# Shared feed-forward with its features on the partitions, and router products placed between its products

## The reference

```python
# x: (16, 512, 256)
h = layernorm(x)
a = tanh(h @ WA.T); b = h @ WB.T              # 16 states
g = sigmoid(h @ Wg.T + bg); dx = h @ WD.T + bD
hs = scan(h_t = a_t * h_{t-1} + b_t)          # along the 512 tokens
x = x + (hs @ WC.T) * g + dx * (1 - g)

h2 = layernorm(x)
shared = (silu(h2 @ shared_gate_w) * (h2 @ shared_up_w)) @ shared_down_w   # 256 -> 256 -> 256
p, idx = top_k(softmax(h2 @ router_w), 2)     # 16 experts
routed = sum over the 2 chosen experts e of  p_e * (silu(h2 @ gate_w[e]) * (h2 @ up_w[e])) @ down_w[e]
out = x + routed + shared
```

## Time and profile before

| | |
|---|---|
| median of 3 runs | 772.59 us (772.11 to 775.65) |
| span of the profiled execution | 772.7 us (no time of its own is noted beside it) |
| part A, from the first gate product to the first transposed expert rows | 14.96 to 429.97 us |
| halves with front, back and tail | 14, from 61.60 to 388.40 us |
| TensorE (PE) busy | 601.8 us (78%) |
| VectorE (DVE) busy | 539.9 us (70%) |
| ScalarE (ACT) / GpSimd (POOL) busy | 321.6 / 368.3 us |
| mean granted TensorE clock | 0.918 of full |

### The profile page before, as it was taken

One profiled execution on the slowest core, in us unless ns is written; L12 is line 12 of the kernel. 1 busy time (PEld: TensorE's weight loads), 2 busy tenths in 40 slices (PEclk: granted clock), 3 DMA queues, 4 the chain that ended last, 5 costly groups with the idle time before them and its releaser, 6 DMA issues.

```text
span 772.7 us, 16380 instructions
## 1 busy us (share of the span) xinstructions
PE 601.8 (78%) x3710; PEld 499.9 (65%) x3741; DVE 539.9 (70%) x1660; ACT 321.6 (42%) x733; POOL 368.3 (48%) x516
## 2 busy tenths in 40 slices
PE   3689899999999999999974788988988988970000
PEld 2467777777778777778763677877877877750000
DVE  8778898888899988897866245545445444545776
ACT  4366455565555565555452233333333333330000
POOL 3214445654545644445647356556556656661000
PEclk9789999999999999999997699999999999995555
DMA  4994111110101111101114434434544444417998
GB/s 155 275 330 125 38 40 50 56 48 34 48 34 56 55 41 41 48 34 57 57 45 171 117 120 156 155 114 155 156 131 148 146 135 146 147 50 247 379 385 293
DMA packets 82806, 96.91 MB, mean 125 GB/s; under 512 B 10142, under 2 KB 74066, under 8 KB 82774
## 3 DMA queue, kind: packets, MB, share of 16 engines
q1 hardware_dynamic: 61270, 54.32, 23.3%
q0 software_dynamic: 13056, 33.84, 12.1%
q10 hardware_dynamic: 8448, 8.39, 3.1%
HBM read 52.04 MB, written 46.57 MB: 128 GB/s over the span
## 4 chain that ended last, share of the span: by engine, by line
PE 57%; issue 12%; DVE 9%; DMA 7%; ACT 3%; POOL 2%; SPq 1%; DVEq 1%; POOLq 0%; ACTq 0%
PE gd L600 14%; PE tr L398 8%; PE gu L405 5%; DMA raw_w<-expert_results 5%; PE tr L405 5%; PE gd L436 5%; PE dn L405 5%; PE gu L617 4%; PE dn L617 4%; PE cb L398 3%; PE misc L405 2%; PE misc L527 2%; DVE tokens L1293 1%; SPq L383 1%; DMA expert_rows<-row_buf,slot 1%
## 5 line engine op out<-in xcount | busy, mean ns | idle before, releaser
L1355 POOL DMA_INDIRECT expert_rows<-row_buf,slot x128 | 132.0, 1031 | 145.3 <-DVE slot L1011 107.2
L1423 POOL DMA_INDIRECT expert_results<-raw_w,row_ids x144 | 141.6, 983 | 67.9 <-issue 35.2
L600 PE MATMUL gd<-w_hi,bx 128*128 x576 | 112.0, 297 | 0.6 <-DVE bx L1235 0.6
L436 PE MATMUL gd<-wgd,xT 128*128 128x512 f32 x384 | 103.0, 405 | 4.6 <-DVE xT L936 4.6
L398 PE MATMUL tr<-ident,row_buf 128*128 128x128 f32 x416 | 64.6, 279 | 46.4 <-issue 32.9
L1235 DVE TENSOR_TENSOR bx<-tr,bx 128x512 fp32r<-128x512 f32 x72 | 49.8, 692 | 71.6 <-ACT bx L820 63.7
L398 PEld LDWEIGHTS tr<-ident,row_buf 128*128 128x128 f32 x416 | 49.1, 142 | 64.1 <-issue 57.8
L600 PEld LDWEIGHTS gd<-w_hi,bx 128*128 128x128 f32 x576 | 85.1, 192 | 3.1 <-issue 1.0
L820 ACT ACTIVATE bx<-tr 128x512 fp32r<-128x512 f32 x71 | 42.5, 599 | 101.2 <-PE tr L398 101.2
L436 PEld LDWEIGHTS gd<-wgd,xT 128*128 128x128 f32 x384 | 71.7, 196 | 18.9 <-DVE xT L936 3.1
L1254 DVE TENSOR_TENSOR raw_w<-gd,raw_w 128x256 f32<-128x256 f32 x72 | 30.6, 425 | 64.7 <-ACT raw_w L826 64.7
(11 more groups left out here) (155 smaller groups left out, 1250.0 us busy)
## 6 DMA issues: line engine op xcount, KB each, us to landing
row_buf<-expert_rows SPq DMA_DIRECT2D x144, 130.0 KB, 2.1
raw_w<-expert_results SPq DMA_DIRECT2D x32, 512.0 KB, 10.9
tokens<-in_x SPq DMA_DIRECT2D x16, 512.0 KB, 4.9
out<-tokens ACTq DMA_DIRECT2D x16, 512.0 KB, 7.1
expert_results<-raw_w,row_ids POOLq DMA_INDIRECT x144, 2.4
expert_rows<-fill_rows SPq DMA_DIRECT2D x17, 130.0 KB, 2.6
raw_w<-in_gate_w SPq DMA_DIRECT2D x16, 128.0 KB, 4.3
raw_w<-in_up_w SPq DMA_DIRECT2D x16, 128.0 KB, 4.4
```

Source lines behind the costliest of these rows:

```text
L436: pe.matmul(gd[j % 2][:], xT[a][:, c, j * P:(j + 1) * P], wgd[b][:, c, :], start=(a, b, c) == (0, 0, 0), stop=False)
L600: last = pe.matmul(bgu[p][:, h * 2 * F:(h + 1) * 2 * F], bx[a][:, p, (h * KC + c) * P:(h * KC + c + 1) * P], gate_up_w[b][:, bass.ds(at[h] ...
L1355: pool.indirect_dma_start(out=rows, out_offset=bass.IndirectOffsetOnAxis(ap=slot[:, q, choice, j:j + 1], axis=0), in_=row_buf[:, q, j, :], ...
L1423: pool.indirect_dma_start(out=results, out_offset=bass.IndirectOffsetOnAxis(ap=row_ids[:, at, h:h + 1], axis=0), in_=y[:, w, h, :], in_off ...
```

## The change

The inner values of the shared feed-forward are made with the 256 inner features on the partitions and the 512 tokens of the block moving. Weights are now the stationary operand: `shared_gate(c)` and `shared_up(c)` for the two feature tiles c, six matmuls of 512 columns each. Their product is already transposed for the down product, so the inner transposes go; `inner_hi` (ACT) and `inner_lo` (DVE) split it from the SBUF tile `inner`. Elementwise work goes by 128x512 instead of 128x256. The four down products of a block all run in the next half, two to a bank (`dn`, `gu`), and DVE adds two token tiles at once. In halves with a front the 16 router matmuls (32 columns moving, a 128x128 piece of `h2T` stationary) are issued between the twelve of `shared_gate(0)` and `shared_up(0)`. `ranks_of_block` comes after `shared_gate(1)`, `shared_up(1)` is last. The front transposes of a block are all made in the half before.

```diff
-            def inner_transposes(k, j):
-                pe.wait_ge(inner_ready, J * k + j + 1)
-                if j:
-                    pe.wait_ge(innerT_ready, J * k + j)
-                transposes(cb, 0, [inner[:, j % 2, c * P:(c + 1) * P] for c in range(KC)], th_done)
...
             def shared_down_of(k, j):
-                pe.wait_ge(innerT_ready, J * k + j + 1)
-                if known(k, 1) or j:
-                    pe.wait_ge(shared_added, J * k + j)
-                three_passes(dn[:, 0:D], lambda a, c: innerT[a][:, j % 2, c * P:(c + 1) * P],
+                if j == 0:
+                    pe.wait_ge(innerT_ready, 2 * k + 2)
+                at = (j % 2) * D
+                three_passes(shared_out[j // 2][:, at:at + D], lambda a, c: innerT[a][:, c, j * P:(j + 1) * P],
                              lambda b, c: wshd[b][:, c, :]).then_inc(dn_done, 1)
...
+                def shared_gate(c, between=None):
+
+                    if c:
+                        pe.wait_ge(silu_ready, 2 * k + 1)
+                    elif known(k, 1):
+                        pe.wait_ge(shared_added, 2 * k)
+                    three_passes(gu[:], lambda a, i: wsh[a][:, i, c * P:(c + 1) * P],
+                                 lambda b, i: h2T[b][:, i, :], between).then_inc(gate_done, 1)
+
+                def shared_up(c, between=None):
+
+                    if c:
+                        pe.wait_ge(inner_ready, 2 * k + 1)
+                    elif known(k, 1):
+                        pe.wait_ge(shared_added, 2 * k - 1)
+                    three_passes(dn[:], lambda a, i: wsh[a][:, i, D + c * P:D + (c + 1) * P],
+                                 lambda b, i: h2T[b][:, i, :], between).then_inc(up_done, 1)
...
+                        def with_gate(m):
+                            for step in router[m:m + 1] if m < 4 else router[2 * m - 4:2 * m - 2]:
+                                router_step(*step)
+
+                        def with_up(m):
+                            for step in router[8 + 2 * m:10 + 2 * m] if m < 2 else router[10 + m:11 + m]:
+                                last = router_step(*step)
+                                if step == router[-1]:
+                                    last.then_inc(router_done, 1)
+
+                        shared_gate(0, with_gate)
+                        shared_up(0, with_up)
...
+            def inner_hi(k, c):
+                act.wait_ge(inner_ready, 2 * k + c + 1)
+                if known(k, 1):
+                    act.wait_ge(dn_done, J * k)
+                act.activation(innerT[0][:, c, :], inner[:, c, :], ACT.Copy).then_inc(innerT_hi, 1)
...
+            def inner_lo(k, c):
+                dve.wait_ge(innerT_hi, 2 * k + c + 1)
+                dve.tensor_tensor(innerT[1][:, c, :], inner[:, c, :], innerT[0][:, c, :].bitcast(F32),
                                   ALU.subtract).then_inc(innerT_ready, 1)
...
-            def add_shared(k, j):
-                dve.wait_ge(dn_done, J * k + j + 1)
-                dve.tensor_tensor(tokens[:, J * k + j, :], tokens[:, J * k + j, :], dn[:, 0:D],
+            def add_shared(k, g):
+                dve.wait_ge(dn_done, J * k + 2 * g + 2)
+                two = tokens[:, bass.ds(J * k + 2 * g, 2), :]
+                dve.tensor_tensor(two, two, shared_out[g][:].rearrange("q (j d) -> q j d", j=2),
                                   ALU.add).then_inc(shared_added, 1)
...
+                    gate_and_dx_out(1)
                 if back:
                     if known(k, 1):
-                        act.wait_ge(gu_done, J * k)
+                        act.wait_ge(up_done, 2 * k)
                     for g in range(2):
                         act.wait_ge(t2_done, 2 * k + g + 1)
                         turned_out(h2T[0], tr[g], g, h2T_hi)
-                if front:
-                    gate_and_dx_out(1)
-                    gate_and_dx_out(2)
```

More of the change, by code:

```diff
@@ L458, in ranks_of_block, with router_step, back_transposes @@
                     last.then_inc(rank_done, 1)
[L460 to L464, removed]
+                def router_step(j, a, c):
+                    return pe.matmul(misc[:, j * 2 * E:(j + 1) * 2 * E], h2T[a][:, c, j * P:(j + 1) * P],
+                                     wrt[:, c, :], start=a == c == 0, stop=a == 1 and c == KC - 1)
+                def shared_gate(c, between=None):
[12 more added lines that the diff above has]
+                                 lambda b, i: h2T[b][:, i, :], between).then_inc(up_done, 1)
+                def back_transposes(g):
+                    pe.wait_ge(h2_ready, J * k + 2 * g + 2)
+                    if front:
+                        pe.wait_ge(xT_ready, 2 * f + g + 1)
+                    else:
+                        pe.wait_ge(h2T_ready, 2 * k + g - 1)
+                    transposes(tr[g], 0, [row_buf[:, p, 2 * g + h, c * P:(c + 1) * P]
+                                          for h in range(2) for c in range(KC)], t2_done)
                 if front:
@@ L523, in half @@
                         pe.wait_ge(ffn_lo, 3)
-                    for j in range(J):
-                        for a in range(2):
-                            for c in range(KC):
-                                last = pe.matmul(misc[:, j * 2 * E:(j + 1) * 2 * E], h2T[a][:, c, j * P:(j + 1) * P],
-                                                 wrt[:, c, :], start=a == c == 0, stop=a == 1 and c == KC - 1)
-                    last.then_inc(router_done, 1)
-                    shared_gate_up(0)
-                    if not front:
-                        ranks_of_block()
+                    router = [(j, a, c) for j in range(J) for a in range(2) for c in range(KC)]
+                    if front:
+                        def with_gate(m):
[8 more added lines that the diff above has]
+                        shared_up(0, with_up)
+                    else:
+                        for step in router:
+                            last = router_step(*step)
+                        last.then_inc(router_done, 1)
+                        shared_gate(0)
+                        shared_up(0)
                 if front:
@@ L536, in half @@
                 if back:
-                    shared_gate_up(1)
+                    shared_gate(1)
+                if front:
+                    recurrent(3)
+                if back:
+                    ranks_of_block()
                 if last_back:
@@ L1051, in half @@
                 means(0)
+                if tail:
+                    add_shared(k - 1, 0)
+                steps_to_table(s, 11, 13)
                 means(1)
@@ L1160, in half @@
                 if back:
-                    gated_inner(3)
+                    gated_inner(1)
                 next_newton(2)
```

198 lines of the change are left out of this document (68 added, 130 removed).

## The result

The changed kernel takes 784.5 us (median of 4 runs, 782.27 to 788.99) where the kernel before takes 772.35 beside it (4 runs, 771.63 to 775.65): ratio 1.0148, 95% interval 1.0109 to 1.0188. It is slower by 12 us. The forecast was slower by 18. The profiled execution took 783.2 us with a span of 781.4, which is 8.7 more than the 772.7 of before. In every run with both on record the time is 1.7 to 1.9 us above the span. By that the profiled execution of before took some 774.5 us, 2 above its median, so the spans show less of a loss than the medians do.

What follows compares the result with a forecast made beforehand. TensorE was taken to bound the half by little, DVE having about 2 us to spare. 13 halves x 1.4 = 18.2, last half -1, s = 0 +1, rest 0, took 772.7 to 790.9, stated as 791 us; range 774 to 806.

Steps and rivals of the forecast that it cites:

- Router loads: Router matmuls between the shared products: weight loads stay exposed, 0.11 us for each router matmul, a saving of nothing.
- The lap: Middle half laid out in four steps through DVE, TensorE and ACT: from 22.92 to 24.4 us, 1.4 more.
- Steps 1 and 2: Half's start to h2T, then to the router: first h2T split about T+10.2, shared_gate(0) with first router matmul at T+12.8.
- step 3: Interleaved shared and router matmuls up to router_done: 4.58 us plus 0.08 and 0.19, ending T+17.65; DVE waits there.
- step 4: From DVE's logits reduction to the next half: 1.28 + 5.40 + 0.05 us, so next gate_and_dx(0) at T+24.4.
- My reason for the two kinds of half: Middle halves: the slower kind (23.61 us) is slower because DVE pieces wait for POOL's reads, 0.88 instead of 0.42.
- s = -1 and s = 0: Start of part A: half s = 0 has no tail but the same router step, +1 us; s = -1 not costed.
- last half to the first send of block 14's slots: Last of the 14 full halves: no xT split, so its slots come about 1 us earlier, -1.
- rival D: TensorE's new waits bring the lower 1.2 GHz clock in part of the halves: 801 us, or 812 in each; chance 0.14.
- the milder case of D: Lower clock in one half of two, 1 to 1.7 us a time: +10, 801 us; the range's upper end says 806.
- B: Router matmuls nearly vanish, 0.03 us each; half takes 23.1 us, 773 to 776 us, no change; chance 0.13.
- C: Faster: TensorE stays the bound, saved transposes count, 14 x -0.9 = -13 us, 760 us; chance 0.15.

Runs made afterwards that it cites:

- before_start_moved: Kernel before with the change's placing at the start alone (xT's second-half turning and split moved a half earlier for s = -1 and s = 0); 769.51 us, ratio 0.996.
- changed_again: The changed kernel itself, unaltered, run once more on the third chip beside the kernel before; 798.38 us, ratio 1.0137.
- before_router_between: Kernel before with its 16 router products between the six of shared_gate_up(0) instead of ahead of them; 772.63 us, ratio 1.0021.
- before_tanh_early: Kernel before with ACT's tanh of the states moved ahead of h2(0) and h2(1); 780.32 us, ratio 1.0127.
- the best version: Changed kernel with router in one piece ahead of shared_gate(0), y_diff(0) earlier on DVE and tanh earlier on ACT; 766.18 us, ratio 0.9922.
- router_first: Changed kernel with its 16 router products in one piece ahead of shared_gate(0) again; 779.81 us, ratio 1.009.
- router_first_ydiff_early: router_first with y_diff(0) on DVE moved up between the two splits of h2T; 769.46 us, ratio 0.997.
- lap_shortened: the best version with three DVE moves: first xT split, gated_inner(1) and inner_lo(1) earlier; 791.12 us, ratio 1.0054.
- router_in_gate: Changed kernel with all 16 router products between the six of shared_gate(0), none in shared_up(0); 776.18 us, ratio 1.0067.

## Why the prediction was right, and where its sizes were off

**The place of the loss** was right: it is in the middle halves, and it is made of waits between TensorE and DVE. **Router loads** stay exposed: 16 cost 1.81 in one piece, 1.80 three at a time and 0.10 to 0.11 each by ones and twos; the stretch takes 245.66 - 241.19 = 4.47 us against 4.58 to 4.6. The changed kernel's weight loads (PEld) show it directly:

```profile
241.08 0.19 PEld L405 LDWEIGHTS gu<-h2T,wsh 128*128 128x128 f32 x1
241.20 0.19 PEld L457 LDWEIGHTS misc<-wrt,h2T 128*128 128x128 f32 x1
241.43 0.19 PEld L405 LDWEIGHTS gu<-h2T,wsh 128*128 128x128 f32 x1
241.54 0.19 PEld L457 LDWEIGHTS misc<-wrt,h2T 128*128 128x128 f32 x1
241.77 0.19 PEld L405 LDWEIGHTS gu<-h2T,wsh 128*128 128x128 f32 x1
```

The load of the second long matmul starts at 241.43, when the router matmul starts, although the load ahead of it was over at 241.39. The rule of "TensorE: Matmul & The Clock Gate" in the Trainium skill, section "Step-by-step: what each phase is for", that loads are pulled ahead of matmuls in flight, holds in these rows with one load ahead and no more.

**The lap**, step by step in the half from 228.07:

| | laid out | measured |
|---|---|---|
| first h2T split | T+10.2 | T+10.57 |
| end of y_diff(0) | T+12.55 | T+12.85 |
| shared_gate(0) starts | T+12.8 | T+13.12 |
| last router matmul done | T+17.65 | T+17.74 |
| next half | T+24.4 | T+24.34 |
| DVE idle at the reduction | 2 | 1.28 |
| TensorE idle at recurrent(1), gd, down | 1, 1, 1 | 0.88, 0.78, 0.91 |

Steps 1 and 2 came 0.3 us late, step 3 took 0.2 less and step 4 0.1 less; so that the half comes out within 0.1 us owes something to errors that cancel. The twelve halves s = 2 to 13 went from 278.46 to 294.93 us, 1.37 each where 1.4 was forecast. That the order is the cause is shown by taking steps out of it: one step gave back 0.6 to 0.9 us a half, whether it was the router or the scan; the router and y_diff(0) at once gave back 1.4 in the faster kind of half and 0.6 in the slower. Together they give back 12.9 of the 16.5 us that the twelve halves had lost. What keeps the other 3.6, be it the DVE pieces of 512 columns or something else, was not taken apart. The idle time at the reduction fell short by 0.7. Of that 0.3 is the lateness of steps 1 and 2, and 0.36 I had in the rows: DVE's y_gated(1) was held up beside POOL in the changed kernel as well (0.79 us instead of 0.43). My reason for the two kinds of half was wrong: the piece of 0.88 in the earlier trace rows stands in the faster half, and the slower one from 250.87 has only one such piece (0.97) where the faster has two.

**The terms that were mis-sized** are those of the ends. The sum against the trace:

| term | forecast | measured |
|---|---|---|
| halves s = 1 to 13 | +18.2 | +16.5 for s = 2 to 13, -2.8 for s = 1 |
| s = -1 and s = 0 | +1 | +0.2 (start), -3.5, -1.5 |
| last half to the first send of block 14's slots | -1 | +1.0 |
| from there to the end of part A | 0 +- 3 | 0 |
| part B | 0 | -1.2 |
| span | +18.2 | +8.7 |

Of the 9.5 us between forecast and trace, 5.8 are the start and 4.2 the half s = 1; the last half has the wrong sign (it takes 23.12 us instead of 21.83), which takes back 2.0. As to the start, I costed "s = 0: +1" and said nothing of s = -1, although the diff moves the second xT split out of the half that needs it there too. Before, that half began with waits of 2.67 and 1.41 us for two xT splits in turn; in the changed kernel the splits are both made ahead:

```profile
33.98 2.14 PE L432 MATMUL gd<-wgd,xT 128*128 128x512 f32 x6 [2.10 <-DVE xT L931]
```

before_start_moved confirms 3.5 us of it; the rest of the start's 4.8, 1.3 us, is less than the start differs by between two executions of the changed kernel (s = 1 at 56.80 and, in changed_again, at 58.70). The -2.8 of s = 1 is of another kind: before's half there ran at a mean clock of 0.94, and the changed kernel's does not. I had used that half's rows only as evidence for rival D, and then costed the half as if it were an ordinary one. But most of it is no gain of the change: in before_router_between and before_tanh_early the half s = 1 takes 24.03 and 23.90 us at a clock of 1.00, so about 2.5 us of it belong to the one execution of before that was profiled. I had also set that execution's span equal to the median time (772.7 and 772.6), though it must have taken some 774.5. Both put the loss by spans, 8.7, below the loss by medians, 12. The upper end of the range, 806, is called the milder case of D, which the text puts at 801; nothing hung on it.

**The rivals.** B fell with before_router_between. C had a true core: with the router, y_diff(0) and the tanh all moved, the twelve middle halves are faster than before's, by 1.7 us together and not by the 0.9 a half that C wanted. D did not come in the changed kernel (1.00 in the full halves, both times), but in three kernels made from it.

## What to carry to other kernels

When two engines are nearly full and hand work to each other, don't add up busy times: lay the new order out as one lap, from an instruction back to itself in the next round, and look for what in it can move up without lengthening another step; here one ACT instruction was worth 10 us. But ask for each such move when its input arrives, for the same move cost 9 us in the kernel before, where the input came late. Cost the first and the last rounds from their own rows, since they hold waits that the middle ones do not have. And before you credit a gain to the middle, sum the middle rounds by themselves: the best version won more over the kernel before in its start than in its twelve middle halves.

## What the runs showed of the hardware

**A DVE piece beside a POOL read.** A piece of 256 columns whose inputs both lie in SBUF takes 0.42 us, and 0.65 to 1.31 where it meets POOL's addition x+dx. The slow one in the earlier trace rows started at 245.95; POOL's row in the trace of before:

```profile
245.83 0.73 POOL L1351 TENSOR_TENSOR xdx<-tokens,dx 128x256 f32<-128x256 f32 x1 [0.51 <-ACT dx L701]
```

It ends at 246.56, and the DVE piece 0.27 us behind that. For the 0.93 of router_first the same distance is 0.29, and for the 1.31 of router_first_ydiff_early too, though that piece began 0.28 us ahead of POOL's addition, while a row send of POOL (257.36 to 258.32) was still running. "SBUF — State Buffer" in the Trainium skill, section "SBUF: two separate sides", says that such a piece and a GpSimd instruction that reads SBUF exclude one another for the whole instruction, and that the one that starts first has the way. The rows agree for the most part: these pieces are not slowed in proportion, their end hangs on the end of POOL's addition. But the piece of 1.31 had begun first and was held up as well, and the one of 0.66 at 259.96 ended 0.59 us before the end of the addition beside it, which took 0.95 us instead of 0.74. How many pieces are hit goes with the kind of half in the versions with the new products: in the changed kernel one piece (0.79) in the half of 24.34 us and three (1.17, 0.65, 0.72) in that of 25.02; in router_first_ydiff_early one and three, 22.93 and 24.45 us. With all three moves it is one piece of 0.65 in the half of 23.01 and none in that of 22.63; there DVE waits for POOL's result instead (0.71 and 1.18 us). It is at most part of the explanation, since in the kernel before the faster kind has two such pieces (0.89, 0.88) and the slower one (0.97).

**The clock.** Of the full halves s = 1 to 14, stretches at 1.2 GHz stood in five of router_first (s = 1, 3, 4, 13 and 14), six of lap_shortened (s = 4, 5, 6, 8, 10 and 11), one of router_in_gate (s = 14; the mean granted clock from 378.00 to 385.00 is 0.57) and one of the kernel before (s = 1), and in none of the changed kernel, both times, or of the other versions. Waits of TensorE alone don't tell them apart: the changed kernel has three of 0.8 to 0.9 us in a half and no such stretch. router_first and router_in_gate differ only in whether the 16 short matmuls stand in one piece directly behind such a wait, and have five and one; yet router_first_ydiff_early and before_start_moved have them in one piece and show none. Each count is of one execution, that of the changed kernel of two. What triggers a stretch is left open.
